# Wide heads: the products that make the next v, moved ahead of the products of the probabilities with v

## The reference

```python
qh = (q_in @ wq + bq).reshape(b, q_len, H, K)          # H 16, K 128
kh = (kv_in @ wk + bk).reshape(b, t, H, K)
vh = (kv_in @ wv + bv).reshape(b, t, H, K)
kh, vh = concat(kh, bias_k), concat(vh, bias_v)        # one learned key and value: 257
weights = softmax(einsum('bqhk,bthk->bhqt', qh, kh) / sqrt(K))
x = x + einsum('bhqt,bthk->bqhk', weights, vh).reshape(b, q_len, H * K) @ wo + bo
```

## Time and profile before

| | us |
|---|---|
| median of three runs | 1519.94 |
| the profiled execution's own time | 1520.21 |
| its span in the trace | 1518.4 |
| TensorE busy (PE) | 1448.6, 95% |
| VectorE busy (DVE) | 968.1, 64% |
| ScalarE busy (ACT) | 890.9, 59% |
| first and last weight load of `times_v` | 275.7 and 996.0 |

### The profile page before, as it was taken

One profiled execution on the slowest core, in us unless ns is written; L12 is line 12 of the kernel. 1 busy time (PEld: TensorE's weight loads), 2 busy tenths in 40 slices (PEclk: granted clock), 3 DMA queues, 4 the chain that ended last, 5 costly groups with the idle time before them and its releaser, 6 DMA issues.

```text
span 1518.4 us, 28583 instructions
## 1 busy us (share of the span) xinstructions
PE 1448.6 (95%) x9712; PEld 1109.0 (73%) x9712; DVE 968.1 (64%) x3358; ACT 890.9 (59%) x2807; POOL 207.1 (14%) x260
## 2 busy tenths in 40 slices
PE   7999999999999999999999999999899998999997
PEld 5766688877787777678778777778666666876664
DVE  4777822556666556456556665631999996158997
ACT  5878933534444433344434443433899997279996
POOL 2010032100100001110010100021212322012200
PEclk9999999999999999999999999999999999999999
DMA  7000012010010101001001000100100100000000
GB/s 299 2 2 2 20 46 91 1 49 16 1 49 16 49 15 35 30 1 49 16 6 59 1 1 1 36 1 1 56 2 9 36 16 8 1 1 9 16 3 22
DMA packets 10879, 40.65 MB, mean 27 GB/s; under 512 B 2416, under 2 KB 2672, under 8 KB 8688
## 3 DMA queue, kind: packets, MB, share of 16 engines
q1 hardware_dynamic: 10736, 38.82, 7.1%
HBM read 37.77 MB, written 1.05 MB: 26 GB/s over the span
## 4 chain that ended last, share of the span: by engine, by line
PE 63%; ACT 18%; issue 5%; DVE 2%; POOL 1%; POOLq 0%; DVEq 0%; ACTq 0%
ACT probs L1099 12%; PE bank L923 8%; PE bank L904 7%; PE bank L888 7%; PE bank L937 7%; PE bank L865 6%; ACT pT L1107 5%; PE bank L878 5%; PE bank L809 5%; PE bank L798 5%; PE bank L912 4%; PE bank L643 2%; PE bank L627 1%; PE bank L952 1%; PE bank L832 1%
## 5 line engine op out<-in xcount | busy, mean ns | idle before, releaser
L1099 ACT ACTIVATE probs<-probs,negmax 128x256 f32<-128x256 f32 (+1 forms) x640 | 349.4, 559 | 41.3 <-DVE negmax L1376 40.5
L1189 ACT ACTIVATE pT<-bank 128x512 f32<-128x512 f32 x128 | 76.4, 597 | 395.9 <-PE bank L912 395.9
L643 PEld LDWEIGHTS bank<-ident,probs 128*128 128x128 f32 x1536 | 168.4, 141 | 118.3 <-ACT probs L1099 59.9
L643 PE MATMUL bank<-ident,probs 128*128 128x128 f32 x1536 | 226.5, 281 | 27.9 <-ACT pT L1107 16.6
L1521 DVE TENSOR_REDUCE stats<-bank 128x1 f32<-128x257 f32 x256 | 107.0, 424 | 148.4 <-PE bank L904 147.4
L1376 DVE CUSTOM_DVE_ANT_0 probs<-bank,mask_a 128x256 f32<-128x256 f32 (+1 forms) x384 | 173.8, 508 | 28.2 <-PE bank L627 23.4
L1107 ACT ACTIVATE pT<-bank 128x512 f32<-128x512 f32 x288 | 171.1, 595 | 7.1 <-PE bank L643 7.0
L923 PE MATMUL bank<-pT,probs 128*128 128x256 f32 x512 | 136.3, 389 | 9.9 <-ACT pT L1189 8.2
L1099 ACT ACTIVATION_READ_ACCUMULATOR probs<-probs,negmax 128x1 f32 x640 | 132.6, 207 | 0.0
L1180 ACT ACTIVATE probs<-bank,stats 128x257 f32<-128x257 f32 x256 | 118.8, 474 | 4.6 <-DVE stats L1524 3.7
L923 PEld LDWEIGHTS bank<-pT,probs 128*128 128x128 f32 x512 | 92.7, 190 | 33.7 <-ACT pT L1189 17.3
(11 more groups left out here) (195 smaller groups left out, 2656.6 us busy)
## 6 DMA issues: line engine op xcount, KB each, us to landing
w_m<-in_w SPq DMA_DIRECT2D x6, 1024.0 KB, 6.9
g_qkv<-in_g SPq DMA_DIRECT2D x4, 1536.0 KB, 6.4
q_res<-in_g SPq DMA_DIRECT2D x4, 1536.0 KB, 6.5
w_qkv<-in_w SPq DMA_DIRECT2D x3, 768.0 KB, 4.4
g_bv<-in_gbv SPq DMA_DIRECT2D x8, 256.0 KB, 4.3
g_o<-in_go SPq DMA_DIRECT2D x4, 512.0 KB, 3.3
q_res<-in_go SPq DMA_DIRECT2D x4, 512.0 KB, 3.5
rows<-in_rows SPq DMA_DIRECT2D x1, 1664.0 KB, 14.0
```

The costliest lines, as they stand in the source:

```text
L643: last = nc.tensor.transpose(out[:, n * P:(n + 1) * P], probs[:, u % PROBS, q * T + t * P:q * T + (t + 1) * P], ident[:, :])
L1099: last = nc.scalar.activation(s, s, ACT.Exp, bias=negmax[:, u % PROBS, k:k + 1], scale=-1.0, accum_out=sums[:, tile % 2, q, j * c.res + r: ...
```

## The change

`times_v(n)` goes behind `values(u + 1, h - 1)`. Only TensorE's order in the rows with h = 1 and h = 2 of the units 0 to 14 is touched, which is 30 rows in each of the two cross attentions. No instruction is added or removed, and no wait is changed, but the waits in front of `values` now stand in front of `times_v` too.

```diff
                         learned_weights(b)
-                    times_v(n)
                     if h in (1, 2) and u + 1 < UNITS:
                         if h == 1 and u == 0:
                             rows_turned(pe, before, B - 1)
...
                         if h == 1 and u > UNITS - B:
                             pe.wait_ge(sem("d_tout"), st.at("d_tout", 0, u - (UNITS - B)))
                         values(u + 1, h - 1)
+                    times_v(n)
                     if n >= 1:
                         project(n - 1)
```

## The result

The changed kernel takes 1525.10 us, the median of 12 runs, beside 1520.89 for the kernel before on the same chip: ratio 1.0028, 95% interval 1.0020 to 1.0036. That is 4.2 us slower (3.0 to 5.5 by the interval) where 4.1 were forecast, and inside the range. The profiled execution took 1523.82 us.

A forecast was written before the change was run, and what follows sets the result against it. TensorE, busy 95% of the span, was taken as the bound, so only its bubbles count: 30 rows x 0.20 = +6.0, less 1.92 in rows 57, is +4.1 us on 1519.94, giving 1524.0 us; range 1520.8 to 1527.5.

The forecast's parts named there:

- The moved products cost nothing by themselves: times_v and values on TensorE: 0.86 and 1.72 us in the chain, no gap at either seam, so swapping them costs nothing.
- Rows with h = 1 up to row 53: 0: 28 rows: times_v ends 1.72 us later, but VectorE's next maxima keep a 0.26 us margin, so nothing is delayed.
- The second rival (VectorE slips): Rows with h = 1: the 0.26 us margin before the maxima is too small; 0.2 us over it gives 1529.6 us; 8%.
- comes back in full: VectorE lateness beyond the margin in rows with h = 1: every 0.1 us returns whole at the next row's line 1516.
- Rows with h = 2: +0.20 us each: 28 rows, 2 to 54: line 888 waits for VectorE's read of bank 7, ending 0.20 us after ScalarE's copy.
- Rows 57: -0.96 each: Row 57 (h = 1), one per attention: values covers the wait for ScalarE's copy, gaining 0.96 us, twice.
- Rows 58: +0.20 each: Row 58 (h = 2), one per attention: values waits for line 1516, ending 600.00 against 599.80; +0.20 us, twice.
- The sum, +4.1: Both wide attentions: +6.0 us from 30 rows with h = 2 and -1.92 from rows 57, together +4.1 us.
- The first rival (bank 7 is free in time, -6.3 us): The 30 rows with h = 2: bank 7 is read in time, gaps close, -6.3 us, 1513.6 us; 6%.
- The third rival (the wait is cheaper than its record): Rows with h = 2: bank released earlier or loads pass the wait; losses halve to 0.1 us, 1521.0 us; 16%.

The follow-up runs named there:

- read_early: The changed kernel, with VectorE reading the first half of v out of bank 7 in the row with h = 1 instead of h = 2: 1515.41 us, ratio 0.9960.
- slip_h1_more: The changed kernel with three unused VectorE copies (two 128x256, one 128x512) ending rows with h = 1, units 0 to 13: 1531.47 us, ratio 1.0072.
- slip_h1: The changed kernel with two unused 128x256 VectorE copies at the end of rows with h = 1, units 0 to 13: 1524.85 us, ratio 1.0022.
- h2_only: The kernel before, with the order of times_v and values changed in rows with h = 2 alone: 1527.68 us, ratio 1.0046.
- h1_only: The kernel before, with the order of times_v and values changed in rows with h = 1 alone: 1518.46 us, ratio 0.9987.
- late_new: The changed kernel with one unused 128x256 VectorE copy ahead of the read of bank 7 in rows with h = 2: 1529.78 us, ratio 1.0061.

## Why the prediction was right, step by step

- **The moved products cost nothing by themselves.** Right: read_early has the new order and wins 6.30 us.
- **Rows with h = 1 up to row 53: 0.** Right, and the margin is real: forecast 0.26 us, the profile has 0.28. The second rival (VectorE slips) is a true mechanism that did not come into play: slip_h1_more shows its price, slip_h1 that a small lateness beyond the visible idle time is free. The prediction's "comes back in full" was too strong: of 0.38 us beyond the margin 0.27 came back.
- **Rows with h = 2: +0.20 us each.** Right in place and releaser, and in size for 22 of the 28: these are 0.20 us longer. The other six are 0.29 us longer (below). h2_only, with these rows and rows 58 alone, has +6.50.
- **Rows 57: -0.96 each.** Right: h1_only gives -1.92 for two, and the rows themselves are 0.95 us shorter each.
- **Rows 58: +0.20 each.** Line 888 waits there 1.13 us, as forecast (1.1), and the row is 0.21 us longer.
- **The sum, +4.1; measured 4.58 in the two attentions, 4.2 in the runs.** The missing 0.5 is in six of the rows with h = 2, those in which the next unit opens a new group of weights (u = 3, 7, 11). There the program has a second semaphore wait in front of line 888, for the new weights, and the load comes 0.12 us after the end of line 1516 instead of 0.05, with 0.51 us idle instead of 0.42. Six times 0.09 is 0.5. That the second wait is the reason is read from the program and was not tested. The terms of the sum fit one by one, to 0.02 us outside these six rows, so the total is not right by errors that cancel. The timeline of the changed kernel, one of the six, and row 58:

```profile
352.52 0.69 DVE L1516 TENSOR_TENSOR probs<-bank,g_bv 128x512 f32<-128x512 f32 x1
...
353.33 0.30 PEld L888 LDWEIGHTS bank<-q_res,ctxT 128*128 128x128 f32 x2 [0.51 <-issue]
...
602.09 0.30 PEld L888 LDWEIGHTS bank<-q_res,ctxT 128*128 128x128 f32 x2 [1.13 <-DVE probs L1516]
```

- **The first rival (bank 7 is free in time, -6.3 us).** It did not come about here, and its arithmetic is right: read_early makes its condition true and measures -6.30.
- **The third rival (the wait is cheaper than its record).** Wrong. Line 888's load comes 0.05 us after the end of line 1516 (0.12 in the six rows), never before. The rule of the Trainium skill that I weighed (TensorE: Matmul & The Clock Gate, section Architectural detail: weight loads are pulled ahead of matmuls in flight) does not reach past such a wait in any row seen here. Loads that are not held do start ahead of their matmul, most by 0.21 us, as in the kernel before:

```profile
501.75 0.41 PEld L878 LDWEIGHTS bank<-hT,q_res 128*128 128x128 f32 x2
501.96 0.59 PE L878 MATMUL bank<-hT,q_res 128*128 128x256 f32 x2
```

## What to carry to other kernels

An order that closes one wait can uncover another that the moved work had been hiding: before moving work, ask of every instruction that comes forward what released it so late that nobody noticed, and compare the two release times. Here they were 0.20 us apart. That difference in 30 rows, less the 0.95 us that each of the two rows 57 gained, was the forecast; the 0.5 us that it missed lie in six of them, where the load came later behind its release. When an instruction on one engine is moved, move its partner on the other engines too (the read of the bank it needs): the two moves together gave -6.3 us, one alone +4.6 and the other 0.

## What the runs showed of the hardware that was not expected

In the six rows with a second semaphore wait in front of the weight load of line 888, the load came 0.12 us after the end of the releasing instruction instead of 0.05 (0.51 us idle against 0.42), in the changed kernel and in h2_only; whether the second wait is the cause was not tried. A copy of 128x256 f32 in SBUF lasts 0.28 us on VectorE, but the next instruction starts 0.20 us after it did (late_new); one of 128x512 lasts 0.42 us, and the next starts 0.33 us after it (slip_h1_more). Two 128x257 maxima take 0.75 us back to back and 0.86 when the second waits for its own scores, so 0.11 us of lateness before them is free in this kernel.
